# Order of work around the joint between the second attention and the local attention of a four-part block

## What is computed

```python
x = x + L0_xattn(ctx, ctx, layernorm(x))     # 16 heads of 8, relative positions
x = x + L0_ffn(layernorm(x))                 # fake-quantised gated feed-forward
# second attention: 16 heads of 8; keys and values from ctx
q = layernorm(x) @ wq.T + bq; k = ctx @ wk.T + bk; v = ctx @ wv.T + bv
x = x + (softmax(q k^T / sqrt(8)) v) @ wo.T + bo
# local part on z = layernorm(x), two layers, 8 heads of 64, window 64:
h = shift_token(z); q, k, v = split(h @ wqkv, 3)
q, k = l2norm(q) * qs, l2norm(k) * ks; q, k = rotary_xpos(q, k)
z = z + local_attention(q, k, v) @ wo
z = z + (a * gelu(g)) @ w2 + b2              # a, g from layernorm(shift_token(z)) @ w1
out = x + z
```

## Time and profile before

| What | Value |
|---|---|
| Median of three runs | 429.11 us (429.06 to 431.6) |
| Profiled execution, own time | 431.58 us |
| Its span, first to last instruction | 429.8 us |
| Mean granted TensorE clock in it | 0.956 of full speed |
| TensorE, VectorE, ScalarE busy | 86%, 81%, 67% of the span |

### The profile page before, as it was taken

One profiled execution on the slowest core, in us unless ns is written; L12 is line 12 of the kernel. 1 busy time (PEld: TensorE's weight loads), 2 busy tenths in 40 slices (PEclk: granted clock), 3 DMA queues, 4 the chain that ended last, 5 costly groups with the idle time before them and its releaser, 6 DMA issues.

```text
span 429.8 us, 10211 instructions
## 1 busy us (share of the span) xinstructions
PE 371.4 (86%) x4104; PEld 272.0 (63%) x4104; DVE 349.4 (81%) x721; ACT 289.1 (67%) x602; POOL 22.8 (5%) x30
## 2 busy tenths in 40 slices
PE   2799999998556789997858999999999999997866
PEld 1488788886511435564435766876767687776845
DVE  5989978986888899886979889888797988884642
ACT  1789998884355457778354666867868777766641
POOL 2000020000020040000000000000000002020110
PEclk9999999999955999999999899999999999998997
DMA  8700010000000000000000000000000000000000
GB/s 325 302 4 4 3 41 3 3 4 3 1 0 1 2 0 2 2 2 0 2 1 2 0 2 0 2 2 0 2 2 1 2 0 2 2 0 2 25 2 24
DMA packets 1774, 8.30 MB, mean 19 GB/s; under 512 B 192, under 2 KB 448, under 8 KB 1472
## 3 DMA queue, kind: packets, MB, share of 16 engines
q1 hardware_dynamic: 1728, 7.65, 4.5%
HBM read 7.12 MB, written 0.52 MB: 18 GB/s over the span
## 4 chain that ended last, share of the span: by engine, by line
PE 48%; DVE 32%; ACT 14%; issue 5%; DMA 1%; DVEq 0%; ACTq 0%
PE ps L252 13%; PE ps L657 5%; ACT blk L1350 3%; PE ps L505 3%; DVE blk L1180 3%; PE ps L630 3%; DVE blk L1171 3%; DVE blk L1162 3%; PE ps L611 2%; PE ps L569 2%; DVE lneg L1187 2%; DVE ss L1172 2%; PE ps L621 2%; PE ps L583 2%; PE ps L492 2%
## 5 line engine op out<-in xcount | busy, mean ns | idle before, releaser
L569 PE MATMUL ps<-w_f,full 128*128 128x512 f32 x96 | 44.7, 599 | 1.4 <-issue 0.9
L1468 ACT ACTIVATE PT<-ps,lneg 128x128 f32<-128x128 f32 x128 | 34.6, 381 | 13.9 <-DVE lneg L1187 13.9
L630 PEld LDWEIGHTS ps<-blk,PT 128*128 128x128 f32 x256 | 30.3, 192 | 0.6
L630 PE MATMUL ps<-blk,PT 128*128 128x65 f32 x256 | 30.4, 272 | 0.0
L252 PEld LDWEIGHTS ps<-blk,st 128*128 128x128 bf16 x768 | 26.8, 98 | 3.8
L1162 DVE TENSOR_TENSOR blk<-ps,tabs 128x1024 f32<-128x1024 f32 x16 | 19.5, 1221 | 11.5 <-ACT blk L1435 11.2
L252 PE MATMUL ps<-blk,rel 128*128 128x64 bf16 x768 | 27.6, 193 | 0.0
L252 PE MATMUL ps<-blk,st 128*128 128x64 bf16 x768 | 27.6, 193 | 0.0
L569 PEld LDWEIGHTS ps<-w_f,full 128*128 128x128 f32 x96 | 16.9, 190 | 16.9 <-issue 16.7
L1022 DVE TENSOR_REDUCE mneg<-ps 128x4 bf16<-128x512 bf16 x32 | 21.9, 686 | 6.6 <-PE ps L357 6.4
L583 PEld LDWEIGHTS ps<-const,blk 128*128 128x128 f32 x128 | 14.8, 146 | 17.3 <-DVE blk L1180 14.6
(11 more groups left out here) (235 smaller groups left out, 913.9 us busy)
## 6 DMA issues: line engine op xcount, KB each, us to landing
w_f<-f_dram SPq DMA_DIRECT2D x2, 1689.0 KB, 13.3
w_x<-l_dram SPq DMA_DIRECT2D x1, 774.0 KB, 6.0
w_f<-ffn_dram SPq DMA_DIRECT2D x1, 561.0 KB, 8.0
X<-x_dram SPq DMA_DIRECT2D x1, 512.0 KB, 3.6
ctxT<-ctxT_dram SPq DMA_DIRECT2D x1, 512.0 KB, 4.5
OT<-maskT_dram SPq DMA_DIRECT2D x1, 512.0 KB, 7.1
rest<-l_dram SPq DMA_DIRECT2D x1, 385.0 KB, 4.2
const<-const_dram SPq DMA_DIRECT2D x1, 324.0 KB, 6.3
```

Of the source, the lines that this page charges most:

```text
L569: m = mm(ps[:, c, :], hT[:, n, :], w_f[:, l, F_QKV + 512 * c:F_QKV + 512 * (c + 1)], start=True, stop=True)
L630: m = mm(ps[:, 5 + h // 4, 65 * (h % 4):65 * (h % 4 + 1)], P1[:, i % 2, P * h:P * (h + 1)], VL[:, i % 3, s, :], start=(h % 4 == 0), stop=T ...
L1468: e = a(S1[:, i % 2, P * k:P * (k + 1)], ps[:, 3 + c, P * j:P * (j + 1)], ACT.Exp, bias=lneg[:, i % 2, k:k + 1])
```

## The change

Eight edits, in three groups. TensorE: in step n = 5 `turn_second_o(0)` and `project_second_o(0)` each come half a step sooner; `turn_first_z` goes from n = 7 to n = 6; `qkv(0, 0, 2)` goes ahead of `turn1(14)`; `turn_back(4)` goes from n = 6 to n = 7 and `turn_back(5)` behind `qkv(1)`; `unread(8, 4)` becomes `unread(4, 4)`. VectorE: the addition of the projection and the moments go from after unit 13 to between the maximum and the subtraction of unit 12, the normalisation from after unit 14 to after unit 12; `divide_batch(4)` goes behind `rotate(0)`; `largest(0)` goes ahead of `divide_batch(6)` and `unit_norm(1)`. ScalarE: `take_output(1, 0)` goes ahead of the exponential of unit 11, `norm_root(5)` from unit 14 to unit 12, `take_turned_z(0)` from unit 15 to unit 14, `square(0)` ahead of the exponential of unit 15, `take_batch(7)` behind `square(1)` and `take_v(1)`. The waits of `turn_back` and `turn_first_z` follow the new order of bank 7's users.

```diff
@@ -524,15 +524,13 @@
                 if n >= 1:
                     pe.wait_ge(sem("o_norm"), 4 + n)
                 if n == 4:
-                    pe.wait_ge(sem("res_added"), 5)
-                if n == 5:
                     pe.wait_ge(sem("zT"), 1)
                 for k in range(G):
                     i = tr(ps[:, 7, P * k:P * (k + 1)], OU[:, n % 2, P * k:P * (k + 1)], ident)
                 i.then_inc(sem("o_back"), 1)
 
             def turn_first_z():
-                pe.wait_ge(sem("o_norm"), 9)
+                pe.wait_ge(sem("res_added"), 5)
                 for n in range(4):
                     pe.wait_ge(sem("z_in"), n + 1)
                     i = tr(ps[:, 7, n * P:(n + 1) * P], Z[:, n, :], ident)
@@ -710,33 +708,32 @@
             for n in range(NB):
                 if n + 1 < NB:
                     scores1(n + 1, 0)
+                if n == 7:
+                    pe.wait_ge(sem("f_in"), 32)
+                    qkv(0, 0, 2)
                 turn1(2 * n)
-                if n == 6:
+                if n == 5:
+                    turn_second_o(0)
+                if n == 7:
                     turn_back(4)
-                if n == 7:
-                    turn_first_z()
                 if n >= 1:
                     weigh1(2 * n - 1)
                 if n == 5:
-                    turn_second_o(0)
-                if n == 7:
-                    pe.wait_ge(sem("f_in"), 32)
-                    qkv(0, 0, 2)
+                    project_second_o(0)
                 if n + 1 < NB:
                     scores1(n + 1, 1)
                 turn1(2 * n + 1)
+                if n == 6:
+                    turn_first_z()
                 if n == 7:
                     qkv(0, 2, 3)
                 weigh1(2 * n)
-                if n == 5:
-                    project_second_o(0)
-                if n == 7:
-                    turn_back(5)
                 if 1 <= n <= 4:
                     turn_back(n - 1)
             weigh1(2 * NB - 1)
             qkv(1)
-            unread(8, 4)
+            turn_back(5)
+            unread(4, 4)
             turn_qk(0)
             turn_back(6)
             unread(3, 4)
@@ -1131,21 +1128,20 @@
                 s = ps[:, 2 * (u % 2):2 * (u % 2) + 2, :].rearrange("p b (h k) -> p (b h) k", k=P)
                 dve.wait_ge(sem("scores1"), u + 1)
                 step(v.tensor_reduce(m1[:, u % 2, :], s, AX.X, ALU.max))
+                if u == 12:
+                    add_projection(1, 0)
+                    moments(5, X, 0, 4)
                 settle()
                 if u >= 2:
                     dve.wait_ge(sem("turned1"), 2 * (u - 1))
                 v.tensor_tensor(S1[:, u % 2, :].rearrange("p (h k) -> p h k", h=HG), s,
                                 m1[:, u % 2, :].rearrange("p (h o) -> p h o", o=1).to_broadcast([P, HG, P]),
                                 ALU.subtract).then_inc(sem("less_max"), 1)
-                if u == 13:
-                    add_projection(1, 0)
-                    moments(5, X, 0, 4)
-                    divide_batch(4)
                 if u in (5, 7, 9):
                     divide_batch((u - 5) // 2)
                 elif u == 10:
                     divide_batch(3)
-                elif u == 14:
+                elif u == 12:
                     normalise(5, X, Z, "z_in", 0, 4)
 
             heads = lambda t: t.rearrange("p (s h j) -> p s h j", s=2, h=LH)
@@ -1229,13 +1225,16 @@
                 normalise(7 + q, O, Y, "y", 2 * (q % 4), 2 * (q % 4) + 2)
 
             rotate(0)
+            divide_batch(4)
             unit_norm(0)
             divide_batch(5)
             rotate(1)
+            largest(0)
             divide_batch(6)
             unit_norm(1)
             for i in range(2 * NB):
-                largest(i)
+                if i >= 1:
+                    largest(i)
                 if i == 0:
                     divide_batch(7)
                 if i >= 5 and i % 2 == 1:
@@ -1519,27 +1518,27 @@
                         if w >= 2:
                             act.wait_ge(sem("weighed1"), w - 1)
                         a(P1[:, w % 2, 512 * c:512 * (c + 1)], ps[:, 4 + c, :], ACT.Copy).then_inc(sem("pt1"), 1)
+                if u == 11:
+                    take_output(1, 0)
+                if u == 12:
+                    norm_root(5)
                 if u == 14:
-                    norm_root(5)
-                if u == 15:
                     act.wait_ge(sem("h_zeroed"), 1)
                     take_turned_z(0)
+                if u == 15:
+                    act.wait_ge(sem("local_zeroed"), 1)
+                    square(0)
                 if u < U:
                     act.wait_ge(sem("less_max"), u + 1)
                     a(S1[:, u % 2, :], S1[:, u % 2, :], ACT.Exp, scale=SOFT).then_inc(sem("exp1"), 1)
                 if u >= 3 and u % 2 == 1:
                     take_batch((u - 3) // 2)
-                if u == 11:
-                    take_output(1, 0)
-                if u == 15:
-                    act.wait_ge(sem("local_zeroed"), 1)
-                    square(0)
                 if u == 16:
                     take_v(0)
-            take_batch(7)
             head_root(0)
             square(1)
             take_v(1)
+            take_batch(7)
             take_turned_qk(0)
             head_root(1)
             for i in range(2 * NB):
```

## The result

The changed kernel takes 427.17 us (median of 13, 425.66 to 430.18); the kernel before, run beside it, 430.03 us (median of 13, 428.95 to 431.6). The ratio is 0.9942 with a 95% interval of 0.9922 to 0.9961, so 1.7 to 3.4 us sooner. That 427.17 comes within 0.5 us of the forecast of 427.6 is in part luck: the forecast started from 429.11, a median of three, and the median of 13 is 0.9 higher; from there a saving of 1.5 would have given 428.5.

A forecast was written before the change was run, and what follows sets the result against it. The prediction took the kernel to be bounded by tiles 0 and 1 passing one after another through VectorE. From 429.1 us, -2.3 for the maximum and +0.8 for the first half gave 427.6, range 425.3 to 430.0.

The forecast's parts named there:

- What bounds the kernel: From 203.6 to 223.3, tile 0 and tile 1 go one after another through VectorE; no engine is full.
- The first half: Work moved sooner ahead of rotate(0): moves of 2 to 3 us shrink to 0.6, then rotate(0) starts 0.8 later.
- The term +0.8: rotate(0) starts at 204.4, 0.8 us later than before, because square(0) waits for ScalarE's copies of unit 14.
- The bound "if the copies did not come between": Without unit 14's copies ahead of it, square(0) would start at 201.9 and rotate(0) at 203.0, 0.7 sooner than before.
- The bound of 3.5 us sooner: If only VectorE's own work stood in its way, rotate(0) would start at 200.1, 3.5 us sooner.
- The maximum: The first maximum starts directly after rotate(1) instead of 2.30 later, behind unit_norm(1): -2.3 us.
- Its cover: score(0) is done at 216.5, 0.9 us before rotate(1) ends at 217.4, so the first maximum need not wait.
- the rival that the move gives nothing: turn_qk(1), 2.0 later, decides the following tile, so the 2.3 comes back as waiting: about 429.3 us, chance 0.10.
- The sum: -2.3 from the first maximum and +0.8 from the first half give -1.5 us, carried from rotate(2) to the end.
- The forecast's own range: 426.2 to 428.8 us around the forecast 427.6, described as half the bounds of the first part.
- The rival of a fall after the new stop: TensorE idles from 203.6 to 205.4, then runs at 1.2 GHz; rotate(1) 1.9 later than forecast: 429.5 us, chance 0.15.
- the full payment of the first half: Rival: rotate(0) starts when VectorE is free, 3.5 us sooner; with the 2.3 the time is 423.3 us, chance 0.10.

The follow-up runs named there:

- square_first: The changed kernel with square(0) ahead of the two copies of unit 14 on ScalarE: 426.23 us, ratio to the kernel before 0.9907.
- max_alone: The kernel before with one edit, largest(0) ahead of divide_batch(6) and unit_norm(1): 426.64 us, ratio to the kernel before 0.9915.
- before_filled: The kernel before with six unread matmuls ahead of turn_qk(2), in TensorE's stop at 232.3 to 234.2: 430.37 us, ratio 1.0003.
- first_half_alone: The changed kernel with the first maximum put back behind unit_norm(1): 430.69 us, ratio to the kernel before 1.0013.
- unread_8: The changed kernel with four unread matmuls put back, 8 instead of 4 ahead of turn_qk(0): 428.62 us, ratio to the kernel before 0.9957.
- before_again: The kernel before, unchanged, profiled once more for its half-clock stretches: 430.05 us in one execution.
- before_filled_at_222: The kernel before with eight unread matmuls ahead of turn_second_o(1), in TensorE's stop at 221.3 to 224.2: 430.04 us, ratio 0.9995.
- add_and_square: The changed kernel with the addition behind the subtraction of unit 12 and square(0) ahead of unit 14's copies: 425.93 us, ratio to the kernel before 0.9905.

## Why the prediction was right, and where it was off

**What bounds the kernel** held: the chain through VectorE from rotate(0) to rotate(2) is in both profiles, and each shift of the first maximum went one for one through to the fourth and on to the fourteenth wherever no half-clock stretch cost time between. A shift of rotate(0) did not always: the 1.35 of square_first were 0.83 at rotate(1).

**The first half** was read rightly in its mechanism. Addition predicted 188.2, measured 188.19; subtraction of unit 12 190.35, 190.32; scores of unit 14 191.6, 191.60; turned Z 198.6, 198.35; square(0) 203.35, 203.05. The moves of 2 to 3 us did shrink to under 1 and then turn into a loss, and two experiments showed the two places: the subtraction held back, and square(0) behind the copies. The term +0.8 was mis-sized: it measured +0.51. The steps between 192 and 198 were taken a little too long: 0.16 by the transposes of unit 13 (196.85 against 196.69) and 0.12 more by turn_first_z (197.9 against 197.62). The bound "if the copies did not come between" put rotate(0) at 203.0; square_first measured 202.97. The bound of 3.5 us sooner is not consistent in itself: it has rotate(0) at 200.1, while the same paragraph has VectorE free at 200.7 (200.32 in the trace: 204.11 less 3.79 idle), which leaves 2.9 to 3.3.

**The maximum** was forecast at -2.3 and measured -2.37. Its cover held: in the changed kernel's timeline the last matmuls of score(0) run from 214.69 to 215.85, 1.1 ahead of the maximum at 216.98.

```profile
214.69 1.16 PE L252 MATMUL ps<-blk 64*128 64x128 f32 x16
```

The later unit_norm(1) did not decide; the rival that the move gives nothing is refuted by max_alone, whose fourth maximum keeps all of the gain.

**The sum** was -1.5 and the order of work gives 63.85 - 65.73 = -1.88. In the two profiled executions shown the spans differ by 4.6: 1.88 order, 1.47 the half-clock stretch at 236.0 to 239.4, 1.2 the tail. The prediction had called that stretch "probably" part of the 2.47 by which the profiled execution lay above the median; by the ruler it is 1.47. The forecast's own range, 426.2 to 428.8, is called half the bounds, but does not come out of halving them; it holds the measured 427.17.

**The term left out.** The prediction let the median move by the order of work alone. The measured ratio's middle is 2.5 us, though 1.88 lies inside its interval; for max_alone the interval (2.6 to 4.7 us) excludes the 2.38 of order. The rest, 0.6 us for the changed kernel and 1.3 for max_alone, goes with a higher granted clock; that the clock causes it is argued, not shown. The nearest candidate is the stretch at 236, which costs 1.47 where it falls: TensorE's stop ahead of turn_qk(2), 1.92 in the kernel before, is 1.5 in the changed kernel and in max_alone. Filling either stop in the kernel before did not bring the gain, though before_filled could hide it (see there), and only one or two profiles of each kernel show where stretches lie. The rival of a fall after the new stop (1.81 us, 203.26 to 205.07) did not appear in any profile of a kernel with that stop; one of the changed kernel's 13 executions, 430.18 us at a clock of 0.956, has no trace to look at. That the full payment of the first half did not come is shown by first_half_alone.

## What to carry over

Work moved ahead in one queue gains nothing where the engine that must pass it on is in order behind something that the same move has delayed; follow the moved result to its last consumer before counting a microsecond. A reduction whose inputs are ready and whose result starts another engine goes ahead of work that only the next round needs. Compare two orders by the distance between fixed instructions in the timeline, not by spans or few medians, when stretches of half clock differ between executions.

## What was not expected of the hardware

The stretches at half clock (1.2 GHz) that fall after 185 us while TensorE still has work lasted 3.4 or 6.8 us, and their number differs between executions of one and the same kernel. The profiles of unread_8 and square_first have none. The first profile of before has one at 236, one at 390 and a double one (6.8 us) at 417; before_again has one at 224, a double one at 388 and one at 418.

In the tail, the part from the fourteenth to the sixteenth maximum took 24.6 without one, 25.4 to 25.7 with one and 26.6 to 26.7 with a double one; the part after the sixteenth 29.4 without, 30.9 to 31.1 with one and 32.4 with a double one. So a stretch of 3.4 us costs 0 to 1.7 us by where it lands, and the tail alone spreads these profiles over 3.9 us.

TensorE's stop of 2.95 us (it begins between 221.3 and 222.2) went with half clock in three of the four profiles that have it (before_again, before_filled, first_half_alone): the clock fell between 0.6 us before its end and 1.0 after. Only two profiles have the stop of 1.9 us ahead of turn_qk(2), the first of before and before_filled_at_222; half clock followed in the first alone. The tail tells the same. All twelve profiles have a stop of 2.8 us before 391 us and one of 1.84 between 409 and 417; half clock came with each of the two in ten profiles and with neither in unread_8 and square_first. The stop of 2.8 us in two kernels, add_and_square and unread_8, granted clock third from the end:

```profile
382.00:383.00 1.00, 0.00 (x0) 0.00 (x0) 0.93 (x4) 1.00 (x5) 0.00 (x0) 1.00 0.00 0
383.00:384.00 1.00, 0.00 (x0) 0.00 (x0) 0.93 (x3) 1.00 (x5) 0.00 (x0) 0.75 0.00 0
384.00:385.00 1.00, 0.38 (x2) 0.39 (x3) 0.93 (x4) 0.08 (x1) 0.00 (x0) 0.50 0.00 0
```

```profile
386.00:387.00 1.00, 0.00 (x0) 0.00 (x0) 1.00 (x2) 0.48 (x2) 0.00 (x0) 1.00 0.00 0
387.00:388.00 1.00, 0.99 (x9) 0.99 (x10) 0.89 (x5) 0.00 (x0) 0.00 (x0) 1.00 0.00 0
```

So the same stop can cost the clock or not; what decides it no run here shows.

The Trainium skill (TensorE: Matmul & The Clock Gate, section "HAM oscillation — how this bites in real kernels") says that waits between bursts of matmuls let the clock drop, with an example whose waits are longer than these stops. Three of the four profiles with the stop of 2.95 us agree that a pause can do it; the fourth has full clock behind the same stop.
